# Attention logits: block-by-block weights, and exp straight from PSUM on ScalarE

## The chip, the cores and the metric

The kernel runs on one core of one Trainium2 chip. The metric is the device time of one launch in microseconds (us); smaller is better. TensorE (PE in the rows, PEld for its weight loads), VectorE (DVE), ScalarE (ACT) and GpSimd (POOL) each run their own list of instructions in order and wait for each other by semaphores. The queue that SyncE issues DMAs from is SP.

## The reference, cut to what matters

A batch of 64 images becomes 65 tokens each, 128 text tokens are joined to them (193 tokens, written L), and one attention block with relative positions and one feed-forward block follow. What the change touches is this part of the attention (8 heads, 8 channels each for q and k):

```python
rel_idx = arange(L)[:, None] - arange(L)[None, :] + (L - 1)
rpe = rel_emb[:, rel_idx]
logits = (einsum('bhdi,bhdj->bhij', q, k) + einsum('bhdi,dij->bhij', q, rpe_k)
          + einsum('bhdi,dij->bhij', k, rpe_q))
attn = softmax(logits, axis=3)
out = einsum('bhij,bhdj->bhdi', attn, v) + einsum('bhij,dij->bhdi', attn, rpe_v)
```

## The kernel before

A first stage turns the images into tokens. The second stage, `fused_block`, handles the 32 pairs of images, one pair to a turn of a loop, as a software pipeline: the table `SCHEDULE` is one list of step names that every engine walks through. In a turn, the steps "c", "a", "w2t" belong to the feed-forward of one pair, "log", "exp", "tr", "rel", "pv", "place" to the attention of the next pair, and "proj" to "gaff" (projections and their group norm) to the pair after that. A step "c" is one of 16 feed-forward slices: three matmuls of 386 columns on TensorE, a product on VectorE, two gelus on ScalarE, a sum on GpSimd, and, three slices late, two more passes on TensorE. Its first matmul waits until ScalarE has done the first gelu of the slice two before it.

The logits of a pair are made in 25 blocks. The 128 output rows of a block are 16 (image, head) pairs times 8 query rows, so both products need block-diagonal weights: `q_bd` (q of one head in 8 partitions, zeros elsewhere) and `a_bd` (q and k values spread so that each query row meets its own shift of the position table `rw`). In the kernel before, block o holds the query rows o, o+25, ..., and its weights are the slice `q_bd[:, :, o::OCT]`, which has a stride of 25 elements (100 bytes). `log` i computes blocks 2i and 2i+1 into one of two PSUM banks; VectorE takes each row's maximum and writes the difference to `lp` in SBUF; four `exp` steps on ScalarE turn `lp` into exponentials in place. Then `tr` transposes groups of four blocks on TensorE and VectorE and ScalarE copy one half each.

The block-diagonal tiles are filled by DMAs of the SP queue (`spread`): k and q are written to a DRAM scratch, 16 DMAs copy q's heads into `q_bd`, and 8 DMAs read the scratch back into the diagonal places of `a_bd`, whose other places stay zero. It starts when the step `gaff` of the turn before has written `q_f` and `k_f`. The first `log` waits for all of them.

Of the kernel before, what the change touches and what calls it, by code (L numbers as in the profile page):

```python
# [51 lines left out]
LP = 8 * OCT  # L52
RW = OCT - 1 + L
GRP = 4
# [17 lines left out]
_at = 0  # L72
for _n, _w in (("ident", P), ("ones", P), ("g8", P), ("g4", P), ("mask_r", 8), ("place", HD + HD + HD)):
    CO[_n] = (_at, _w)
    _at += _w
# [8 lines left out]
SCHEDULE = (  # L84
# [12 lines left out]
N_QS, N_AS = 16 * BH, 16 * 8  # L97
EXP_AT = (0, 8, 14, 20, OCT)


def is_first(t):
    return isinstance(t, int) and t == 0


def resident(nc, ctx):

    sb = lambda n, s: ctx.enter_context(nc.sbuf_tensor(n, s, F32))
    return dict(
        con=sb("con", [P, NCONST]),
        wq_z=sb("wq_z", [P, 192]),  # L110
        wk_z=sb("wk_z", [P, 192]),
        wv_s=sb("wv_s", [P, P]),
        vec=sb("vec", [P, 16]),
        pos_s=sb("pos_s", [P, 1 + NPATCH]),
        wg_s=sb("wg_s", [P, E]),
        b1_s=sb("b1_s", [P, NF]),
        b2_s=sb("b2_s", [P, E]),
        rv=sb("rv", [P, 2 * OCT * P]),
        w2_s=sb("w2_s", [P, NF, P]),
        rw=sb("rw", [P, RW]),  # L120
        const_in=ctx.enter_context(nc.semaphore("const_in")))
# [5 lines left out]
def patch_embed(nc, a, tok_scratch, R):  # L127

    with ExitStack() as ctx:
# [75 lines left out]
        def _(act):  # L205
# [58 lines left out]
def fused_block(nc, txt, w1, tok_scratch, u_scratch, out, R):  # L264

    with ExitStack() as ctx:
# [25 lines left out]
        gst, gst_o = (sb(n, [P, 7, 4]) for n in ("gst", "gst_o"))  # L292
        q_bd = sb("q_bd", [P, BH, LP])
        a_bd = sb("a_bd", [P, BH, LP])
        mx = sb("mx", [P, 32])
# [22 lines left out]
        bank = [ctx.enter_context(nc.psum_tensor(f"bank{i}", [P, 512], F32)) for i in range(8)]  # L318
        zb, yb, lg, pv, misc = bank[0:2], bank[2], bank[3:5], bank[5:7], bank[7]

        LN = {"1": (misc, e1, e2, rs1, rs1_t), "2": (pv[0], t1, t2, rs2, rs2_t)}

        names = """w1_in w1_hi_ready w1_split setup_dve setup_pool setup_act tok_in txt_t h_ready qk_ready v_ready
            bn mv_ready gmean gspread gvar gve grstd affine_part affine norm q_spread a_spread u_out log_ready max_done log_done
            vt v_copied exp_done tr_ready tr0_copied tr1_copied wm_done pv_done pv_ready rec_done o_part obn omv omean ospread ovar ove orstd oaff_part oaffine
            onorm h2_ready logits top_done dl_ready e_ready e1_ready p1_ready ep_tr ep_copied bcast_ready
# [53 lines left out]
        def _(sp):  # L380
# [5 lines left out]
            def spread(t):  # L386
# [40 lines left out]
        def _(pe):  # L427
# [58 lines left out]
            def attend(s, t):  # L486
# [35 lines left out]
                elif s[:3] == "log":  # L522

                    i = int(s[3:])
                    if i == 0:
                        pe.wait_ge(S["q_spread"], t * N_QS + N_QS)
                        pe.wait_ge(S["a_spread"], t * N_AS + N_AS)
                    elif i >= 2:
                        pe.wait_ge(S["log_done"], t * FILLS + i - 1)
                    for k in range(2 if 2 * i + 1 < OCT else 1):  # L530
                        o = 2 * i + k
                        dst = lg[i % 2][:, k * 256:k * 256 + L]
                        mm(dst, q_bd[:, :, o::OCT], k_f[:, 0:L], start=True, stop=False)  # L533
                        m = mm(dst, a_bd[:, :, o::OCT], rw[:, OCT - 1 - o:OCT - 1 - o + L], start=False, stop=True)  # L534
                    m.then_inc(S["log_ready"], 1)
                elif s[:2] == "tr":

                    g = int(s[2])
                    octs = range(g * GRP, min(OCT, (g + 1) * GRP))
                    pe.wait_ge(S["exp_done"], t * 4 + sum(octs[-1] >= x for x in EXP_AT))  # L540
                    for c, (j0, jn) in enumerate(JC):
                        if g == 0:
                            pe.wait_ge(S["log_done"], t * FILLS + FILLS)
                        else:
                            pe.wait_ge(S[f"tr{c}_copied"], t * NG + g)
# [21 lines left out]
                elif s[:3] == "rel":  # L567
# [7 lines left out]
                    for o in octs:  # L575
                        part = pv[g % 2][:, (o - octs[0]) * P:(o - octs[0] + 1) * P]
                        mm(part, rv_o[:, 0, o, :], pr[0][:, o, :, :], start=True, stop=False)  # L577
                        m = mm(part, rv_o[0:JC[1][1], 1, o, :], pr[1][0:JC[1][1], o, :, :],  # L578
                               start=False, stop=True)
# [36 lines left out]
        def _(dve):  # L616
# [61 lines left out]
            def reciprocal(b, t):  # L678

                dve.wait_ge(S["pv_done"], t * 2 + b + 1)  # L680
                v.reciprocal(rows(t2, b), by_row(pv[b], 256)).then_inc(S["rec_done"], 1)

            def attend(s, t):
# [33 lines left out]
                elif s == "gaff":  # L717
                    group_affine(4, gst, S["grstd"], S["affine_part"], S["affine"], GS, GB, t)
                elif s[:3] == "log":

                    i = int(s[3:])
                    w = 2 if 2 * i + 1 < OCT else 1
                    if i == 0 and not is_first(t):
                        dve.wait_ge(S["pv_ready"], t * 2)
                    src = lg[i % 2][:, :].rearrange("p (k x) -> p k x", k=2)[:, 0:w, 0:L]
                    dve.wait_ge(S["log_ready"], t * FILLS + i + 1)
                    v.tensor_reduce(mx[:, 2 * i:2 * i + w], src, AX, ALU.max).then_inc(S["max_done"], 1)  # L727
                    dve.wait_ge(S["max_done"], t * FILLS + i + 1)
                    v.tensor_tensor(lp[:, 2 * i:2 * i + w, 0:L], src,
                                    mx[:, 2 * i:2 * i + w].unsqueeze(2).broadcast_to([P, w, L]),  # L730
                                    ALU.subtract).then_inc(S["log_done"], 1)
                elif s[:2] == "tr":
# [15 lines left out]
                elif s in ("place0", "place1"):  # L748
# [86 lines left out]
        def _(act):  # L835
# [19 lines left out]
            def attend(s, t):  # L855
# [11 lines left out]
                elif s == "hkeep":  # L867
# [3 lines left out]
                    a(h2[:, :], h[:, :, :].rearrange("p b l -> p (b l)"), ACT.Copy).then_inc(S["h_kept"], 1)  # L871
                elif s[:3] == "exp":
                    k = int(s[3])
                    o0, o1 = EXP_AT[k:k + 2]
# [28 lines left out]
        def _(pool):  # L903
# [30 lines left out]

            for x in (q_bd, a_bd):
                g.memset(x[:, :, :], 0.0).then_inc(S["setup_pool"], 1)
            pool.wait_ge(S["setup_dve"], 7)
# [13 lines left out]
def shape_constants(np):  # L951
# [11 lines left out]
    put("g4", (p[:, None] // 4 == p[None] // 4) / 4.0)  # L963
    put("mask_r", p[:, None] // HD == np.arange(8)[None])
    w = np.zeros((P, 3 * HD))
    w[:, HD:2 * HD] = p[:, None] % HD == np.arange(HD)[None]
# [39 lines left out]
```

## Time and profile before

| what | value |
|---|---|
| median of 3 runs | 3876.37 us (3875.5 to 3880.21) |
| time of the profiled execution | 3886.44 us |
| its span, first to last instruction | 3884.6 us |
| mean granted TensorE clock | 0.978 of full |
| TensorE busy | 3481.7 us (90%) |
| VectorE / ScalarE / GpSimd busy | 57% / 47% / 31% |

The profiled execution took 10 us more than the median of the unprofiled runs. Busy shares are means over the whole program; which engine sets the pace of a stage is read from the rows of that stage.

### The profile page before, as it was taken

The page shows a single profiled execution, that of the slowest core. Times are in us where ns is not written, and L with a number is a line of the kernel's source. Part 1 is how long each engine was busy: PE and PEld are TensorE (multiplying, and loading weights), DVE is VectorE, ACT ScalarE, POOL GpSimd, SP SyncE. Part 2 cuts the span into 40 slices and gives each one's busy share as a digit, 9 for nine tenths or more (in the row PEclk, how much of TensorE's full clock was granted, in tenths as well). Part 3 has the DMA queues.
Part 4 walks back from the last instruction along what each step waited for, and adds up shares of the span by engine and source line. Part 5 has one row for each costly group of instructions (what it writes and reads, how often), then busy time and mean ns, then how long its engine had stood idle before and what let it go on. Part 6 is the DMA issues. An engine that isn't in the chain of part 4 may idle for free.

```text
span 3884.6 us, 66340 instructions
## 1 busy us (share of the span) xinstructions
PE 3481.7 (90%) x22496; PEld 2907.9 (75%) x22496; DVE 2225.5 (57%) x4469; ACT 1810.0 (47%) x2931; POOL 1190.5 (31%) x1192
## 2 busy tenths in 40 slices
PE   4776899999999999999999999999999999999998
PEld 3665777777777777777777777777777777787776
DVE  6884455555555555555555555555555555555554
ACT  6882244444444444444444444444444444444445
POOL 0000133332233333332233333223333333223335
PEclk9997899999999999999999999999999999999999
DMA  7761000000000000000000000000000000000000
GB/s 191 152 147 34 8 10 9 5 6 9 9 7 9 9 9 9 5 6 9 9 7 9 9 9 8 6 7 9 7 9 9 9 9 8 6 7 9 7 8 5
DMA packets 165392, 79.34 MB, mean 20 GB/s; under 512 B 81631, under 2 KB 163871, under 8 KB 165023
## 3 DMA queue, kind: packets, MB, share of 16 engines
q1 hardware_dynamic: 162946, 72.99, 9.0%
q10 hardware_dynamic: 2416, 5.97, 0.5%
q8 instruction: 17, 0.28, 0.0%
q14 instruction: 13, 0.10, 0.0%
HBM read 60.65 MB, written 14.97 MB: 19 GB/s over the span
## 4 chain that ended last, share of the span: by engine, by line
issue 56%; POOL 21%; PE 10%; DVE 2%; SPq 1%; ACT 1%; POOLq 1%; DMA 0%; ACTq 0%; DVEq 0%
POOL gelu L908 20%; PE bank L434 3%; PE bank L510 1%; PE bank L475 1%; PE bank L463 1%; POOL gst L921 1%; PE bank L533 1%; PE bank L534 1%; PE bank L469 1%; PE bank L443 1%; SPq L393 1%; POOLq L907 1%; ACT gelu L842 1%; PE bank L447 1%; PE bank L444 1%
## 5 line engine op out<-in xcount | busy, mean ns | idle before, releaser
L908 POOL TENSOR_TENSOR gelu<-gelu 128x386 f32<-128x386 f32 x1024 | 1031.0, 1015 | 2116.6 <-ACT gelu L842 2110.2
L841 ACT ACTIVATE gelu<-bank,b_s 128x386 f32<-128x386 f32 x1024 | 595.6, 582 | 1334.4 <-DVE gelu L626 1328.2
L434 PE MATMUL bank<-gelu,w_s 128*128 128x386 f32 x2048 | 832.5, 493 | 31.8 <-POOL gelu L908 28.5
L626 DVE TENSOR_TENSOR gelu<-bank,ratio 128x386 f32<-128x386 f32 x1024 | 564.1, 555 | 465.7 <-PE bank L447 459.9
L842 ACT ACTIVATE gelu<-gelu,b_s 128x386 f32<-128x386 f32 x1024 | 623.6, 609 | 0.0
L443 PE MATMUL bank<-x_hi,w_hi 128*128 128x386 f32 x1024 | 523.5, 511 | 51.5 <-ACT gelu L841 47.7
L533 PE MATMUL bank<-k_f,q_bd 128*128 128x193 f32 x1600 | 510.5, 401 | 48.4 <-DMA a_bd<-u_scratch 48.4
L533 PEld LDWEIGHTS bank<-k_f,q_bd 128*128 128x128 f32 x1600 | 463.4, 332 | 69.8 <-DMA a_bd<-u_scratch 39.8
L534 PE MATMUL bank<-rw,a_bd 128*128 128x193 f32 x1600 | 514.0, 403 | 0.0
L727 DVE TENSOR_REDUCE mx<-bank 128x2 f32<-128x386 f32 (+1 forms) x416 | 226.0, 543 | 456.0 <-PE bank L534 456.0
L534 PEld LDWEIGHTS bank<-rw,a_bd 128*128 128x128 f32 x1600 | 460.4, 336 | 0.0
L434 PEld LDWEIGHTS bank<-gelu,w_s 128*128 128x128 f32 x2048 | 364.5, 189 | 79.0 <-POOL gelu L908 54.2
L444 PE MATMUL bank<-x_hi,w_lo 128*128 128x386 f32 x1024 | 348.3, 340 | 0.0
L447 PE MATMUL bank<-x_lo,w_hi 128*128 128x386 f32 x1024 | 347.9, 340 | 0.0
L443 PEld LDWEIGHTS bank<-x_hi,w_hi 128*128 128x128 f32 x1024 | 196.0, 191 | 202.7 <-ACT gelu L841 116.1
L744 DVE TENSOR_TENSOR lp<-bank,con 128x512 f32<-128x512 f32 (+1 forms) x224 | 139.1, 633 | 340.9 <-PE bank L578 340.9
L577 PE MATMUL bank<-probs,rv 128*128 128x128 f32 x1600 | 316.9, 280 | 0.0
L578 PE MATMUL bank<-probs,rv 65*128 65x128 f32 x1600 | 316.0, 279 | 0.0
L547 PE MATMUL bank<-con,lp 128*128 128x128 f32 (+1 forms) x1600 | 227.3, 281 | 68.2 <-ACT probs L881 55.9
L881 ACT ACTIVATE probs<-bank 65x512 f32<-65x512 f32 (+1 forms) x224 | 122.1, 545 | 353.2 <-PE bank L547 353.2
L262 DVE TENSOR_TENSOR xl<-xt,xh 84x1792 fp32r<-84x1792 f32 x64 | 230.1, 3639 | 46.2 <-ACT xh L236 45.4
L547 PEld LDWEIGHTS bank<-con,lp 128*128 128x128 f32 (+1 forms) x1600 | 184.2, 143 | 95.3 <-ACT probs L881 63.3
(146 smaller groups left out, 4901.4 us busy)
## 6 DMA issues: line engine op xcount, KB each, us to landing
xt<-in_x SPq DMA_DIRECT2D x192, 196.0 KB
q_bd<-q_f SPq DMA_DIRECT2D x512, 6.2 KB
a_bd<-u_scratch SPq DMA_DIRECT2D x256, 25.0 KB, 2.2
txt_s<-in_txt SPq DMA_DIRECT2D x32, 128.0 KB, 2.2
rv<-in_rel_v ACTq DMA_DIRECT2D x1, 3200.0 KB, 18.7
u_scratch<-k_f SPq DMA_DIRECT2D x32, 100.0 KB, 2.2
u_scratch<-q_f SPq DMA_DIRECT2D x32, 100.0 KB, 2.2
out<-o_s SPq DMA_DIRECT2D x64, 48.5 KB
```

The source lines that it names most:

```text
L434: mm(yb[:, 0:T2], w2_s[:, f, :], gelu1[:, f % RING, :], start=(f == 0), stop=(f == NF - 1)).then_inc(S["w2_done"], 1)
L443: mm(z, w1_hi[:, w], x_hi[:, :], start=True, stop=False)
L444: mm(z, w1_lo[:, w], x_hi[:, :], start=False, stop=False)
L447: mm(z, w1_hi[:, w], x_lo[:, :], start=False, stop=True).then_inc(S["z_ready"], 1)
L533: mm(dst, q_bd[:, :, o::OCT], k_f[:, 0:L], start=True, stop=False)
L534: m = mm(dst, a_bd[:, :, o::OCT], rw[:, OCT - 1 - o:OCT - 1 - o + L], start=False, stop=True)
L547: m = nc.tensor.transpose(lg[c][0:jn, (o - octs[0]) * P:(o - octs[0] + 1) * P], lp[:, o, j0:j0 + jn], ident)
L577: mm(part, rv_o[:, 0, o, :], pr[0][:, o, :, :], start=True, stop=False)
L626: v.tensor_tensor(gelu2[:, f % RING, :], zb[f % 2][:, 0:T2], ratio[:, :], ALU.mult).then_inc(S["z2_done"], 1)
L841: a(gelu1[:, f % RING, :], zb[f % 2][:, 0:T2], ACT.Gelu, bias=b1_s[:, f:f + 1]).then_inc(S["g_done"], 1)
L842: a(gelu2[:, f % RING, :], gelu2[:, f % RING, :], ACT.Gelu, bias=b1_s[:, f:f + 1]).then_inc(S["g_done"], 1)
L908: g.tensor_tensor(gelu1[:, f % RING, :], gelu1[:, f % RING, :], gelu2[:, f % RING, :], ALU.add).then_inc(S["hs_done"], 1)
```

## The change

The query rows are grouped otherwise: block o now holds rows 8o to 8o+7. `q_bd` and `a_bd` are laid out as [partition, block, (image, head), row], so that the 128 weights of a block lie side by side. `rw` and `rv` get the matching tables. The DMAs for q now write pieces of 8 elements (32 bytes). The 8 DMAs for the shifted values no longer write only the diagonal: each copies all 200 columns to 16 partitions of a new tile `a_rep`, and four products on VectorE (steps `am0` to `am3`, of 7, 6, 6 and 6 blocks) multiply it with a 0/1 mask into `a_bd`. The first `log` waits for all four. The logits use four PSUM banks in place of two. VectorE computes the negated maximum only, and ScalarE computes exp from PSUM block by block with that as bias; the subtraction and the four `exp` steps are gone. In the table of steps, four "c" stand ahead of `am0`, one behind each of `am0`, `am1` and `am2`, none among the `log` steps, and two behind the last `log`.

```diff
 SCHEDULE = (
-    "c c c c c vt0 hkeep log0 log1 log2 c log3 log4 log5 c log6 log7 c log8 "
-    "exp0 log9 exp1 log10 log11 exp2 log12 exp3 c tr0 tr1 rel0 ...
+    "c c c c am0 c am1 c am2 c am3 vt0 hkeep log0 log1 log2 log3 log4 log5 log6 log7 log8 "
+    "log9 log10 log11 log12 c c tr0 tr1 rel0 ...
...
                 for bh in range(BH):
                     rows = slice(DK * bh, DK * bh + DK)
-                    sp.dma_start(q_bd[rows, bh, :], q_f[rows, :]).then_inc(S["q_spread"], 16)
+                    sp.dma_start(q_bd[rows, :, bh, :], q_f[rows, :].rearrange("p (o r) -> p o r", r=8)).then_inc(S["q_spread"], 16)
                 sp.wait_ge(S["u_out"], t * 32 + 32)
                 for r in range(8):
-                    sp.dma_start(a_bd[r:P - 7 + r:8, :, OCT * r:OCT * r + OCT],
-                                 u_scratch[:, :, :, OCT * r:OCT * r + OCT].rearrange("b s d i -> (s d) b i")).then_inc(S["a_spread"], 16)
+                    sp.dma_start(a_rep[r:P - 7 + r:8, :, :], u_scratch[:, :, :, :].rearrange("b s d i -> (s d) b i")).then_inc(S["a_spread"], 16)
...
                     if i == 0:
                         pe.wait_ge(S["q_spread"], t * N_QS + N_QS)
-                        pe.wait_ge(S["a_spread"], t * N_AS + N_AS)
-                    elif i >= 2:
-                        pe.wait_ge(S["log_done"], t * FILLS + i - 1)
+                        pe.wait_ge(S["a_masked"], t * 4 + 4)
+                    elif i >= LOGS:
+                        pe.wait_ge(S["log_done"], t * FILLS + i - LOGS + 1)
...
-                        dst = lg[i % 2][:, k * 256:k * 256 + L]
-                        mm(dst, q_bd[:, :, o::OCT], k_f[:, 0:L], start=True, stop=False)
-                        m = mm(dst, a_bd[:, :, o::OCT], rw[:, OCT - 1 - o:OCT - 1 - o + L], start=False, stop=True)
+                        dst = lt[i % LOGS][:, k * 256:k * 256 + L]
+                        mm(dst, q_bd[:, o, :, :], k_f[:, 0:L], start=True, stop=False)
+                        m = mm(dst, a_bd[:, o, :, :], rw[:, 192 - 8 * o:192 - 8 * o + L], start=False, stop=True)
...
+                elif s[:2] == "am":
+
+                    o0, o1 = (0, 7, 13, 19, OCT)[int(s[2]):int(s[2]) + 2]
+                    if s == "am0":
+                        dve.wait_ge(S["a_spread"], t * N_AS + N_AS)
+                    v.tensor_tensor(a_bd[:, o0:o1, :, :],
+                                    a_rep[:, :, 8 * o0:8 * o1].rearrange("p b (o r) -> p o b r", r=8),
+                                    K["mask_q"].unsqueeze(1).unsqueeze(1).broadcast_to([P, o1 - o0, BH, 8]),
+                                    ALU.mult).then_inc(S["a_masked"], 1)
...
-                    v.tensor_reduce(mx[:, 2 * i:2 * i + w], src, AX, ALU.max).then_inc(S["max_done"], 1)
-                    dve.wait_ge(S["max_done"], t * FILLS + i + 1)
-                    v.tensor_tensor(lp[:, 2 * i:2 * i + w, 0:L], src,
-                                    mx[:, 2 * i:2 * i + w].unsqueeze(2).broadcast_to([P, w, L]),
-                                    ALU.subtract).then_inc(S["log_done"], 1)
+                    v.tensor_reduce(mx[:, 2 * i:2 * i + w], src, AX, ALU.max, negate=True).then_inc(S["max_done"], 1)
...
-                    act.wait_ge(S["log_done"], t * FILLS + (o1 + 1) // 2)
-                    a(lp[:, o0:o1, 0:L], lp[:, o0:o1, 0:L], ACT.Exp).then_inc(S["exp_done"], 1)
+                    act.wait_ge(S["max_done"], t * FILLS + i + 1)
+                    for k in range(w):
+                        o = 2 * i + k
+                        m = a(lp[:, o, 0:L], lt[i % LOGS][:, k * 256:k * 256 + L], ACT.Exp, bias=mx[:, o:o + 1])
+                    m.then_inc(S["log_done"], 1)
```

On VectorE, in the loop's turn, these rows stood between the fourth "c" and the second `log` before (gelu<-bank,ratio is the product of a "c", the rows ISA and REGISTER_ALU only prepare waits):

```order
L626 TENSOR_TENSOR gelu<-bank,ratio 128x386
L624 REGISTER_ALU
L626 TENSOR_TENSOR gelu<-bank,ratio 128x386
L724 ISA
L726 ISA
L727 TENSOR_REDUCE mx<-bank 128x2
L729 TENSOR_TENSOR lp<-bank,mx 128x386
L726 REGISTER_ALU
L727 TENSOR_REDUCE mx<-bank 128x2
L729 TENSOR_TENSOR lp<-bank,mx 128x386
```

And these stand there now, from the fourth "c" to the first maximum:

```order
L623 TENSOR_TENSOR gelu<-bank,ratio 128x386
L720 ISA
L721 TENSOR_TENSOR a_bd<-a_rep,con 128x896
L621 REGISTER_ALU
L623 TENSOR_TENSOR gelu<-bank,ratio 128x386
L721 TENSOR_TENSOR a_bd<-a_rep,con 128x768
L621 REGISTER_ALU
L623 TENSOR_TENSOR gelu<-bank,ratio 128x386
L721 TENSOR_TENSOR a_bd<-a_rep,con 128x768
L621 REGISTER_ALU
L623 TENSOR_TENSOR gelu<-bank,ratio 128x386
L721 TENSOR_TENSOR a_bd<-a_rep,con 128x768
```

The products of the fifth, sixth and seventh "c" stand behind the first mask product, which waits for the DMAs of `a_rep`.

On TensorE, at the third and fourth `log` of the turn, this stood before (L533 and L534 are the two matmuls of a block, L443 to L434 those of a "c"):

```order
L533 MATMUL bank<-k_f,q_bd 128x193
L534 MATMUL bank<-rw,a_bd 128x193
L440 REGISTER_ALU
L443 MATMUL bank<-x_hi,w_hi 128x386
L444 MATMUL bank<-x_hi,w_lo 128x386
L447 MATMUL bank<-x_lo,w_hi 128x386
L433 REGISTER_ALU
L434 MATMUL bank<-gelu,w_s 128x386
L529 REGISTER_ALU
L533 MATMUL bank<-k_f,q_bd 128x193
```

Now the last "c" ahead of the logits, the two transposes of `vt0` and the first block stand so:

```order
L441 MATMUL bank<-x_hi,w_hi 128x386
L442 MATMUL bank<-x_hi,w_lo 128x386
L445 MATMUL bank<-x_lo,w_hi 128x386
L431 REGISTER_ALU
L432 MATMUL bank<-gelu,w_s 128x386
L479 ISA
L481 MATMUL bank<-con,e 128x128
L481 MATMUL bank<-con,e 65x128
L524 ISA
L531 MATMUL bank<-k_f,q_bd 128x193
L532 MATMUL bank<-rw,a_bd 128x193
```

All 50 matmuls of the logits follow each other with no "c" among them.

## Rows read from the trace of the kernel before

**Rows 1.** The page's head: the span and the busy times.

```profile
span 3884.6 us, 66340 instructions
PE 3481.7 (90%) x22496; PEld 2907.9 (75%) x22496; DVE 2225.5 (57%) x4469; ACT 1810.0 (47%) x2931; POOL 1190.5 (31%) x1192
```

**Rows 2.** Costliest groups of the page: count, busy us, mean ns, idle before.

```profile
L841 ACT ACTIVATE gelu<-bank,b_s 128x386 f32<-128x386 f32 x1024 | 595.6, 582 | 1334.4 <-DVE gelu L626 1328.2
...
L626 DVE TENSOR_TENSOR gelu<-bank,ratio 128x386 f32<-128x386 f32 x1024 | 564.1, 555 | 465.7 <-PE bank L447 459.9
```

**Rows 3.** TensorE's waits from 410 to 3880 us: total us, times, longest us.

```profile
PE bank L533 <- DMA a_bd<-u_scratch: 33.4, 31, 3.6
```

**Rows 4.** Timeline of the SP queue: start us, us, form, count.

```profile
2076.09 0.60 SPq L390 DMA_DIRECT2D u_scratch<-k_f  x1
...
2077.37 10.95 SPq L393 DMA_DIRECT2D q_bd<-q_f  x16
2088.44 5.15 SPq L396 DMA_DIRECT2D a_bd<-u_scratch  x8
...
2185.04 0.59 SPq L390 DMA_DIRECT2D u_scratch<-k_f  x1
```

**Rows 5.** Timeline of TensorE at the first logits: start us, us, idle before.

```profile
2095.11 0.80 PE L533 MATMUL bank<-k_f,q_bd 128*128 128x193 f32 x2 [0.87 <-DMA a_bd<-u_scratch]
2095.74 0.64 PE L534 MATMUL bank<-rw,a_bd 128*128 128x193 f32 x2
...
2100.51 0.64 PE L534 MATMUL bank<-rw,a_bd 128*128 128x193 f32 x2
2100.86 0.47 PE L443 MATMUL bank<-x_hi,w_hi 128*128 128x386 f32 x1
...
2102.16 0.56 PE L533 MATMUL bank<-k_f,q_bd 128*128 128x193 f32 x2
```

**Rows 6.** Timeline of TensorE at the projections, whose weights lie side by side.

```profile
2062.88 0.82 PE L510 MATMUL bank<-e,wk_z 128*128 128x193 f32 x4
2063.54 0.81 PE L513 MATMUL bank<-e,wv_s 128*128 128x386 f32 x2
```

**Rows 7.** Timeline of TensorE at the second group of transposes, behind the logits.

```profile
2016.02 0.66 PE L547 MATMUL bank<-con,lp 128*128 128x128 f32 x4 [0.35 <-DVE probs L736]
2018.48 0.65 PE L547 MATMUL bank<-con,lp 128*65 128x128 f32 x4 [1.81 <-ACT probs L881]
```

**Rows 8.** Stretches: us, busy per engine, granted clock, DMA share, GB/s.

```profile
2076.00:2078.50 2.50, 1.59 (x8) 1.03 (x7) 1.20 (x5) 2.50 (x7) 0.59 (x2) 1.00 0.31 81
2089.50:2094.00 4.50, 4.50 (x21) 3.27 (x20) 2.24 (x4) 4.12 (x8) 3.89 (x4) 1.00 0.34 38
100.00:200.00 100.00, 71.34 (x510) 67.29 (x509) 86.75 (x25) 87.14 (x30) 0.00 (x0) 0.91 0.74 154
```

**Rows 9.** Two waits of TensorE and what follows each, same columns.

```profile
333.50:348.40 14.90, 0.00 (x0) 0.00 (x0) 0.00 (x0) 0.85 (x3) 0.00 (x0) 0.50 0.15 19
348.40:351.90 3.50, 3.46 (x11) 3.49 (x12) 0.49 (x1) 0.00 (x0) 0.00 (x0) 0.50 0.02 5
72.00:77.80 5.80, 0.01 (x1) 0.00 (x0) 3.47 (x2) 5.80 (x3) 0.00 (x0) 0.80 0.95 219
77.80:82.20 4.40, 4.37 (x20) 4.38 (x21) 4.40 (x2) 4.40 (x3) 0.00 (x0) 0.50 0.97 197
```

**Rows 10.** VectorE's products by form: busy us, mean ns.

```profile
L744 DVE TENSOR_TENSOR lp<-bank,con 128x512 f32<-128x512 f32 x186 | 128.7, 692 | 332.8 <-PE bank L578 332.8
L646 DVE TENSOR_TENSOR e<-e 128x386 f32<-128x386 f32 x31 | 17.6, 568 | 1.1
```

**Rows 11.** Timelines of GpSimd, then VectorE, at the same moment.

```profile
2073.09 2.93 POOL L908 TENSOR_TENSOR gelu<-gelu 128x386 f32<-128x386 f32 x3
...
2073.24 0.92 DVE L674 TENSOR_TENSOR gst<-gst 128x4 f32<-128x4 f32 x1
```

**Rows 12.** Timeline of ScalarE: two activations of 193 columns out of PSUM.

```profile
2075.95 0.91 ACT L863 ACTIVATE e<-bank,gst 128x193 f32<-128x193 f32 x2
```

More of the change, by code:

```diff
@@ L52 @@
 LP = 8 * OCT
-RW = OCT - 1 + L
+RW = 2 * L - 1
 GRP = 4
@@ L72 @@
 _at = 0
-for _n, _w in (("ident", P), ("ones", P), ("g8", P), ("g4", P), ("mask_r", 8), ("place", HD + HD + HD)):
+for _n, _w in (("ident", P), ("ones", P), ("g8", P), ("g4", P), ("mask_r", 8), ("mask_q", 8), ("place", HD + HD + HD)):
     CO[_n] = (_at, _w)
@@ L292, in fused_block @@
         gst, gst_o = (sb(n, [P, 7, 4]) for n in ("gst", "gst_o"))
-        q_bd = sb("q_bd", [P, BH, LP])
-        a_bd = sb("a_bd", [P, BH, LP])
+        q_bd = sb("q_bd", [P, OCT, BH, 8])
+        a_rep = sb("a_rep", [P, BH, LP])
+        a_bd = sb("a_bd", [P, OCT, BH, 8])
         mx = sb("mx", [P, 32])
@@ L539, in attend @@
                     octs = range(g * GRP, min(OCT, (g + 1) * GRP))
-                    pe.wait_ge(S["exp_done"], t * 4 + sum(octs[-1] >= x for x in EXP_AT))
+                    if g == 0:
+                        pe.wait_ge(S["log_done"], t * FILLS + FILLS)
                     for c, (j0, jn) in enumerate(JC):
-                        if g == 0:
-                            pe.wait_ge(S["log_done"], t * FILLS + FILLS)
-                        else:
+                        if g > 0:
                             pe.wait_ge(S[f"tr{c}_copied"], t * NG + g)
@@ L576, in attend @@
                         part = pv[g % 2][:, (o - octs[0]) * P:(o - octs[0] + 1) * P]
-                        mm(part, rv_o[:, 0, o, :], pr[0][:, o, :, :], start=True, stop=False)
-                        m = mm(part, rv_o[0:JC[1][1], 1, o, :], pr[1][0:JC[1][1], o, :, :],
+                        mm(part, rv[:, (8 * o + P) * HD:(8 * o + P) * HD + P], pr[0][:, o, :, :], start=True, stop=False)
+                        m = mm(part, rv[0:JC[1][1], 8 * o * HD:8 * o * HD + P], pr[1][0:JC[1][1], o, :, :],
                                start=False, stop=True)
@@ L871, in attend @@
                     a(h2[:, :], h[:, :, :].rearrange("p b l -> p (b l)"), ACT.Copy).then_inc(S["h_kept"], 1)
-                elif s[:3] == "exp":
-                    k = int(s[3])
-                    o0, o1 = EXP_AT[k:k + 2]
-                    act.wait_ge(S["log_done"], t * FILLS + (o1 + 1) // 2)
-                    a(lp[:, o0:o1, 0:L], lp[:, o0:o1, 0:L], ACT.Exp).then_inc(S["exp_done"], 1)
+                elif s[:3] == "log":
+                    i = int(s[3:])
+                    w = 2 if 2 * i + 1 < OCT else 1
+                    if i == 0 and not is_first(t):
+                        act.wait_ge(S["pv_ready"], t * 2)
+                    act.wait_ge(S["max_done"], t * FILLS + i + 1)
[3 more added lines that the diff above has]
+                    m.then_inc(S["log_done"], 1)
                 elif s[:2] == "tr":
@@ L933, in attend @@
                     g.tensor_tensor(ep[0:GW, 0:4], half[0:GW, 1:2].broadcast_to([GW, 4]), dl[0:GW, 0:4], ALU.pow).then_inc(S["e_ready"], 1)
-            for x in (q_bd, a_bd):
-                g.memset(x[:, :, :], 0.0).then_inc(S["setup_pool"], 1)
+            g.memset(q_bd[:, :, :, :], 0.0).then_inc(S["setup_pool"], 1)
             pool.wait_ge(S["setup_dve"], 7)
@@ L984 @@
     rel = i["L0_attn_rel_emb"]
-    j_of = np.arange(P)[:, None, None, None] + P * np.arange(2)[:, None, None]
-    rel_rows = np.maximum(OCT * np.arange(8)[:, None] + np.arange(OCT) - j_of + L - 1, 0)
     arrays = {
```

27 lines of the change are left out of this document (12 added, 15 removed), and 2 rows, old and new, of the table SCHEDULE.

## The prediction

> **What bounds the kernel now.** I read the head of the page first [rows 1]: TensorE is busy for 3481.7 of 3884.6 us, the other engines for 57% at most, so over the program TensorE sets the pace. Shares are means, so I then took one turn of the loop from the SP queue's timeline: the scratch of k is written at 2076.09 us and again at 2185.04 us, a turn of 108.95 us [rows 4], and 31 such turns make most of the span. Next the timeline of TensorE at the logits [rows 5]. From 2095.74 to 2100.51 us are ten pairs of passes, two passes to an fp32 matmul, so a matmul starts every 0.477 us; the 50 of a turn take 23.9 us. Nothing waits there: the weights and columns alone set that time. Then the waits [rows 3]: once in each turn, 31 times, TensorE waits for the DMA of `a_bd` ahead of its first logit, for 0.87 us in this turn [rows 5]. So the way of the values through the SP queue is already as long as TensorE's work beside it. Whatever makes this way longer is paid in full, and that is what the reader should keep in mind beside the faster matmuls.
>
> **The change part by part**, in us per turn.
>
> *The 50 logit matmuls.* Their weights had a stride of 100 bytes and lie side by side now. The projections of q and k have the same 193 columns and weights side by side: four passes from 2062.88 to 2063.54 us, 0.165 each [rows 6], against 0.2385 for a pass of the logits. 100 passes take 16.5 in place of 23.9: a gain of 7.4. From below, the gain is nothing if the stride is not what makes them slow; I take 7.4, since size, type and engine are the same in both rows.
>
> *ScalarE and four banks.* Two exps from PSUM have to be done per `log`, which TensorE makes in 8 x 0.165 = 1.32. Two activations of that size from PSUM took 0.91 [rows 12], and the maximum on VectorE takes about 0.55, as a product of 386 columns out of PSUM does [rows 2]. Neither is slower than 1.32, and with four banks TensorE may be three `log` steps, 3.96, ahead of a chain of about 1.5. This costs nothing as long as TensorE covers it; if exp took 0.7 apiece, the logits would run at ScalarE's pace and lose 13 x 0.1 = 1.
>
> *The wait at the second transposes.* TensorE stood for 0.35 and 1.81 there, 2.16 in all [rows 7], since ScalarE had its last long exp, a change of function and two gelus ahead of its copy. Now two "c" stand there. The second covers another 1.30 (the step from 2100.86 to 2102.16 us [rows 5]), but puts two more gelus of 0.58 [rows 2] ahead of the copy, while the exp left over at the end is short. That gives back between nothing and 2.16; I take 0.8.
>
> *The DMAs of q.* 16 issues took 10.95 [rows 4], and their 8 partitions x 25 blocks make 200 pieces of 32 bytes each. The nearest row is that of the old `a_bd` DMAs, 256 pieces of 100 bytes: a DMA share of 0.34 at 38 GB/s [rows 8] is 38/(0.34 x 16) = 7.0 GB/s per busy engine, 14.3 ns apiece. 200 pieces on 16 engines are 0.18, on 8 engines 0.36, under the 0.68 between issues. I take nothing. The upper bound is pieces that cost as much as 800 bytes in the scratch's write: 81/(0.31 x 16) = 16.3 GB/s, 49 ns [rows 8]; on 8 engines that is 1.23 per DMA, 16 x (1.23 - 0.68) = 8.7 in all.
>
> *The DMAs of `a_rep`.* Each moves 16 x 16 rows of 800 bytes, 204.8 KB in place of 25.6. The eight are issued within 5.15 [rows 4], but 1.638 MB have to move. At the rate of the image loads, 154 GB/s at a share of 0.74, that is 208 GB/s [rows 8] and 7.9; at the rate of the scratch's write, 81/0.31 = 261 GB/s, 6.3. The last old one is issued at 2088.44 + 7 x 0.644 = 2092.95 and TensorE starts at 2095.11 [rows 4, 5], 2.16 behind, of which 0.23 is transfer (256 pieces of 14.3 ns on 16 engines). The new ones land at 2088.44 + 1.9 + 7.9 = 2098.2, 3.1 later than before; at the better rate 1.5 later. I take 3.1, since the image loads too write a part of the partitions.
>
> The Trainium skill's page "SBUF — State Buffer" (section "Door 1: The DMA port swizzle") says that a DMA's rate goes by how many of 16 ports its partitions reach, 27.2 GB/s each; by its table, partitions r, r+8, ..., r+120 reach 8. That rule speaks against this change and gives 218 GB/s, an estimate of 7.5 and a landing 2.7 later, where the row gave 3.1; no row here has this pattern of partitions with long pieces.
>
> *The mask products.* Products of 386 and 512 columns take 0.568 and 0.692 [rows 10], about 1 ns per column more, so 896 columns take 1.08 and 768 take 0.95: 3.9 for the four. On VectorE the products of the fifth, sixth and seventh "c" stand among them, 3 x 0.5: together 5.4 from landing to the first logit. They also meet GpSimd's sums: a product of 4 elements took 0.92 while GpSimd ran its sums [rows 11], each about 1.0, so a product with both inputs in SBUF waits until GpSimd's instruction ends. Two of the four can be hit, by the sums of the fifth and sixth "c": 0 to 2, I take 1.2. The first logit starts at 2098.2 + 6.6 = 2104.8.
>
> The same page (section "SBUF: two separate sides") calls the pair of ports that VectorE and GpSimd share an exclusive lock, held for a whole instruction. By that rule GpSimd is held back in turn, and the sixth "c"'s sum could go behind a mask product; the sum stays within my 0 to 2.
>
> *What is queued behind that wait.* VectorE stands at `am0` with the fifth "c" behind it; TensorE can do the fifth and sixth, but the seventh needs the fifth's gelu. Before, the fifth "c" and `vt0` were done 0.87 ahead of 2095.11; a sixth lasts until about 2095.5. Then TensorE has nothing until about 2.4 after the landing, does the seventh, and stands again until 2104.8. Two "c", 2 x 1.30, are now done ahead of the logits, so the 9.7 by which the first logit moves cost 9.7 - 2.6 = 7.1. With the better DMA rate and no sums in the way it is 4.3; with the bound for q's pieces 15.8.
>
> *The clock.* From 2095.5 to 2104.8 us TensorE now works for 1.5 and stands for 7.8. In both waits of comparable or greater length that I list the granted clock was down when work came back: after 14.9 idle it was 0.50 for the first 3.5, after 5.8 idle 0.50 for 4.4 [rows 9], the lower of its two levels, 1.2 GHz. The logits would start at it. A pass of 193 columns is then bound by its columns, so half of some 4.4 is lost: 2.2. Nothing from below, 3.2 from above.
>
> *Sum.* -7.4 - 0.8 + 7.1 + 2.2 = +1.1 per turn, times 31 = +34 us. The first turn has no "c" and pays 3.1 + 3.9 for a gain of 7.4 less the low clock: nothing to speak of. The profiled execution, 3886.4 us, would become 3920; its 10 us over the median 3876.4 taken off, 3910.
>
> **The rivals.**
>
> *The way through the queue grows less, or the clock holds* (faster). Then the matmuls win. With 7.1 and no loss of clock the sum is -1.1, 34 us faster, 3842. With 4.3 and 1.0 for the clock it is -2.9, 90 us faster, 3786. For it: the rate of 261 GB/s is there in the trace, and a wait of 1.81 in every turn leaves the mean clock at 0.978. Against it: the new wait is longer than that one, and the masks cannot start ahead of the last byte. It decides in favour of the change where delay and clock together stay under 8.2.
>
> *Pieces of 32 bytes choke the queue.* At 49 ns on 8 engines the landing moves by another 8.7; at half of the excess 4.3. The sum is +5.4 to +9.8, 167 to 304 us slower, 4045 to 4180. For it: pieces are 25 times as many. Against it: 100-byte pieces ran at 14.3 ns.
>
> *The stride is not what slows the logits.* Then the 7.4 are gone, and the turn loses 8.5 at most: 264 us, 4140. Rows 6 speak against it.
>
> **How the numbers follow.** A measurement of this kernel tells 0.2%, 8 us, from no change. My forecast, a delay that eats the gain, has 0.50, its own range 3860 to 3975; within it 0.08 fall inside 0.2% and 0.02 on the fast side. The faster rival has 0.34, of which 0.01 is within 0.2%. Choked queue 0.11, stride without effect 0.05. Faster: 0.02 + 0.33 = 0.35; same: 0.09; slower: 0.40 + 0.11 + 0.05 = 0.56. The range 3800 to 4000 leaves out about 0.05 of the fastest and 0.13 of the slowest cases.
>
> **What the profile of the changed kernel would show.** Pairs of logit passes 0.33 apart, weight loads no longer as long as a pass. SP's sixteen issues still in 11 us. `am0` starting 22 us after the scratch's write, in place of 19 to the first logit. A wait of TensorE for VectorE ahead of the first logit, and one ahead of the seventh "c" for ScalarE, some 8 us together, with a low clock behind them. Masks near 1 us each, up to 1.9 where GpSimd is in its sum. The wait at the second transposes down to about 1.4. I am wrong if `am0` comes no later than 19 us after the write, if the clock stays up, or if ScalarE, not TensorE, sets the pace of the logits.

## The result, and the profile after

The changed kernel takes 3900.5 us (median of 4 runs, 3891.3 to 3909.3) against 3878.3 us before (4 runs, 3875.5 to 3880.6): ratio 1.0057, 95% interval 1.0032 to 1.0083. It is slower by 22 us or 0.6%, 0.7 us for each of 31 turns. The forecast was 3910 and slower. The profiled execution is the fastest of the four, 3891.3 us with a span of 3889.4. That is 4.8 us over the span of before, whose profiled execution (3886.4 us) was slower than all four of its timed ones.

Head and some groups of the page of the changed kernel (`a_rep` in part 6: KB each, median us from issue to landing):

```profile
span 3889.4 us, 66829 instructions
PE 3295.7 (85%) x22496; PEld 2686.9 (69%) x22496; DVE 2164.7 (56%) x4181; ACT 1953.9 (50%) x3603; POOL 1197.8 (31%) x1191
...
L881 ACT ACTIVATE lp<-bank,mx 128x193 f32<-128x193 f32 x800 | 292.2, 419 | 253.3 <-DVE mx L731 253.3
...
L721 DVE TENSOR_TENSOR a_bd<-a_rep,con 128x768 f32<-128x768 f32 (+1 forms) x128 | 161.7, 1265 | 234.4 <-DMA a_rep<-u_scratch 234.4
...
a_rep<-u_scratch SPq DMA_DIRECT2D x256, 200.0 KB, 4.7
```

TensorE does the same 22496 matmuls in 186 us less busy time than in [rows 1], and the program is not faster: the gain has become waiting. The waits of TensorE in the turns show where (answers to [rows 3]: us in all, times, longest us):

```profile
PE bank L441 <- ACT gelu L841: 264.6, 153, 8.5
...
PE bank L531 <- DVE a_bd L721: 35.1, 31, 1.2
...
PE bank L544 <- ACT probs L887: 21.6, 31, 0.7
```

L441 is the first matmul of a "c". Its large wait comes once in each turn, at the seventh "c". The queue's timeline of one turn, which answers to [rows 4]:

```profile
2080.80 0.59 SPq L389 DMA_DIRECT2D u_scratch<-k_f  x1
...
2082.07 11.89 SPq L392 DMA_DIRECT2D q_bd<-q_f  x16
2094.09 5.15 SPq L395 DMA_DIRECT2D a_rep<-u_scratch  x8
```

VectorE in the same turn, from the fourth "c" to the last mask:

```profile
2097.15 0.56 DVE L623 TENSOR_TENSOR gelu<-bank,ratio 128x386 f32<-128x386 f32 x1 [0.62 <-PE bank L445]
2104.46 1.09 DVE L721 TENSOR_TENSOR a_bd<-a_rep,con 128x896 f32<-128x896 f32 x1 [6.75 <-DMA a_rep<-u_scratch]
2105.47 0.56 DVE L623 TENSOR_TENSOR gelu<-bank,ratio 128x386 f32<-128x386 f32 x1
2105.93 0.95 DVE L721 TENSOR_TENSOR a_bd<-a_rep,con 128x768 f32<-128x768 f32 x1
2106.80 0.56 DVE L623 TENSOR_TENSOR gelu<-bank,ratio 128x386 f32<-128x386 f32 x1
2107.27 1.77 DVE L721 TENSOR_TENSOR a_bd<-a_rep,con 128x768 f32<-128x768 f32 x1
2108.97 0.55 DVE L623 TENSOR_TENSOR gelu<-bank,ratio 128x386 f32<-128x386 f32 x1
2109.44 1.28 DVE L721 TENSOR_TENSOR a_bd<-a_rep,con 128x768 f32<-128x768 f32 x1
```

GpSimd's sums of the fifth and sixth "c" meanwhile (its timeline):

```profile
2107.22 1.01 POOL L914 TENSOR_TENSOR gelu<-gelu 128x386 f32<-128x386 f32 x1 [7.23 <-ACT gelu L842]
2108.56 1.35 POOL L914 TENSOR_TENSOR gelu<-gelu 128x386 f32<-128x386 f32 x1 [0.33 <-ACT gelu L842]
```

And TensorE, which answers to [rows 5]:

```profile
2106.69 0.69 PE L441 MATMUL bank<-x_hi,w_hi 128*128 128x386 f32 x1 [6.66 <-ACT gelu L841]
...
2110.87 0.56 PE L531 MATMUL bank<-k_f,q_bd 128*128 128x193 f32 x2 [1.13 <-DVE a_bd L721]
2111.27 0.49 PE L532 MATMUL bank<-rw,a_bd 128*128 128x193 f32 x2
2111.59 0.49 PE L531 MATMUL bank<-k_f,q_bd 128*128 128x193 f32 x2
...
2127.14 0.48 PE L441 MATMUL bank<-x_hi,w_hi 128*128 128x386 f32 x1
```

The reader is to see the chain: VectorE stands 6.75 us for the last bytes of `a_rep`, with the fifth "c" behind it; TensorE stands 6.66 us for that slice's gelu, and another 1.13 us for the last mask. Then 50 matmuls take 16.27 us, 0.327 apart. From the scratch's write to the first logit are 30.07 us (2080.80 to 2110.87), where 19.02 were. The turn is a usual one: over the 31 turns with a "c" the means are 30.2 and 19.2.

### The profile page after: what moved, and what is told of

Its sections match the earlier page's. It is cut to its first block, busy times and chain, and to the rows that moved or that the text cites. A ratio compares the mean times of both kernels' runs of the same rounds, so it can differ in the third digit from the quotient of the medians.

```text
span 3889.4 us, 66829 instructions
## 1 busy us (share of the span) xinstructions
PE 3295.7 (85%) x22496; PEld 2686.9 (69%) x22496; DVE 2164.7 (56%) x4181; ACT 1953.9 (50%) x3603; POOL 1197.8 (31%) x1191
## 4 chain that ended last, share of the span: by engine, by line
issue 56%; POOL 21%; PE 10%; DVE 2%; SPq 1%; ACT 1%; POOLq 1%; DMA 0%; ACTq 0%; DVEq 0%
POOL gelu L914 20%; PE bank L432 3%; PE bank L508 1%; PE bank L473 1%; PE bank L461 1%; POOL gst L927 1%; PE bank L467 1%; SPq L392 1%; PE bank L441 1%; ACT gelu L842 1%; POOLq L913 0%; PE bank L445 0%; PE bank L442 0%; DVE gelu L623 0%; PE bank L531 0%
## 5 line engine op out<-in xcount | busy, mean ns | idle before, releaser
L432 PE MATMUL bank<-gelu,w_s 128*128 128x386 f32 x2048 | 855.3, 504 | 33.6 <-POOL gelu L914 30.1
L441 PE MATMUL bank<-x_hi,w_hi 128*128 128x386 f32 x1024 | 542.9, 530 | 265.9 <-ACT gelu L841 264.6
L441 PEld LDWEIGHTS bank<-x_hi,w_hi 128*128 128x128 f32 x1024 | 196.5, 192 | 441.8 <-ACT gelu L841 353.4
L531 PE MATMUL bank<-k_f,q_bd 128*128 128x193 f32 x1600 | 405.2, 336 | 58.3 <-DVE a_bd L721 58.3
L432 PEld LDWEIGHTS bank<-gelu,w_s 128*128 128x128 f32 x2048 | 374.4, 194 | 82.3 <-POOL gelu L914 57.4
L881 ACT ACTIVATE lp<-bank,mx 128x193 f32<-128x193 f32 x800 | 292.2, 419 | 253.3 <-DVE mx L731 253.3
L532 PE MATMUL bank<-rw,a_bd 128*128 128x193 f32 x1600 | 401.7, 334 | 0.0
L531 PEld LDWEIGHTS bank<-k_f,q_bd 128*128 128x128 f32 x1600 | 289.7, 195 | 70.0 <-issue 70.0
L721 DVE TENSOR_TENSOR a_bd<-a_rep,con 128x768 f32<-128x768 f32 (+1 forms) x128 | 161.7, 1265 | 234.4 <-DMA a_rep<-u_scratch 234.4
L532 PEld LDWEIGHTS bank<-rw,a_bd 128*128 128x128 f32 x1600 | 290.9, 195 | 0.0
```

The costliest lines, as they stand in the source:

```text
L432: mm(yb[:, 0:T2], w2_s[:, f, :], gelu1[:, f % RING, :], start=(f == 0), stop=(f == NF - 1)).then_inc(S["w2_done"], 1)
L441: mm(z, w1_hi[:, w], x_hi[:, :], start=True, stop=False)
L531: mm(dst, q_bd[:, o, :, :], k_f[:, 0:L], start=True, stop=False)
L532: m = mm(dst, a_bd[:, o, :, :], rw[:, 192 - 8 * o:192 - 8 * o + L], start=False, stop=True)
```

## The experiments

All twelve are told. Times are medians; each ratio is to the kernel before, timed in the same job (3874.1, 3876.8 and 3875.0 us in the three jobs). The changed kernel was not timed again in them, and beside its 3900.5 us the kernel before took 3878.3. So a difference to the changed kernel can be off by some 4 us from that alone: by the ratios, the 28, 18 and 2 us of masks_last, q_whole and warm are 23, 16 and nothing.

**w_side.** The kernel before with weights side by side alone.

```diff
-mm(dst, q_bd[:, :, o::OCT], k_f[:, 0:L], ...)
-m = mm(dst, a_bd[:, :, o::OCT], rw[...], ...)
+mm(dst, q_bd[:, :, :].rearrange("p b l -> p (b l)")[:, P * o:P * o + P], k_f[:, 0:L], ...)
+m = mm(dst, a_bd[:, :, :].rearrange("p b l -> p (b l)")[:, P * o:P * o + P], rw[...], ...)
```

> The kernel before with one edit: the logit matmuls read 128 weights that lie side by side (a flat slice of the same tiles, so the logits are not the reference's; everything else runs as before). Theory A (the stride is what slows them, and the changed kernel loses the gain again elsewhere): matmuls 0.33 us apart instead of 0.477, 7.5 us less per turn, less up to 1.3 since two banks with maximum and subtraction take about as long per step as TensorE: 190 to 230 us faster, 3650 to 3690 us. Rival (stride without effect): 3878 us, no change.

Measured 3681.7 us, ratio 0.9498 [0.9483, 0.9514], 192 us faster. The stride is what made the matmuls slow. TensorE at the logits of this kernel:

```profile
2095.62 0.49 PE L534 MATMUL bank<-rw,a_bd 128*128 128x193 f32 x2
2095.95 0.49 PE L533 MATMUL bank<-k_f,q_bd 128*128 128x193 f32 x2
2096.27 0.49 PE L534 MATMUL bank<-rw,a_bd 128*128 128x193 f32 x2
2096.70 0.59 PE L533 MATMUL bank<-k_f,q_bd 128*128 128x193 f32 x2
```

Matmuls are 0.327 apart within a step, but 0.43 apart where a step begins, about 0.1 us a step or 1.3 us a turn. With two banks TensorE waits there for maximum and subtraction, as I read it; with four banks and no subtraction (both_old_dmas) the gap is gone.

**exp_psum.** The kernel before with the other half alone; the DMAs and the strided weights stay.

```diff
-"c c c c c vt0 hkeep log0 log1 log2 c log3 ... exp0 log9 ... exp3 c tr0 ..."
+"c c c c c c c vt0 hkeep log0 log1 log2 log3 ... log12 c c tr0 ..."
+LOGS = 4;  lt = bank[3:7]      # and maximum, exp and waits as in the changed kernel
```

> The kernel before with the other half alone: negated maximum, exp from PSUM block by block with it as bias, four banks, no 'c' among the logit steps (seven ahead, two behind), old weights and old DMAs. Theory A: costs nothing on TensorE, since ScalarE and VectorE are under its pace; the wait of 0.87 us for the DMAs and half of the wait of 2.16 us at the second transposes go: 1 to 2 us per turn, 30 to 60 us faster, 3820 to 3850 us. Rival (ScalarE's 25 exps cost time): over 3880 us.

Measured 3801.9 us, 0.9815 [0.9799, 0.9832], 72 us faster, more than I expected. The waits show both sources: that for the DMAs, 33.4 us in [rows 3], is 1.0 us here, since two "c" more stand ahead of the logits, and that for ScalarE's copy, 55.9 us before, is 16.4 (us in all, times, longest). The two together are 71.9 us less.

```profile
PE bank L547 <- ACT probs L880: 16.4, 31, 0.5
```

**both_old_dmas.** The two together, with the old DMAs: weights side by side out of `q_bd` and `a_bd` as the old DMAs fill them.

> w_side and exp_psum together on the kernel before, with its old DMAs (the logits are not the reference's): the whole change without the longer way to a_bd. Theory A (the halves add and the loss is all in the way): 3874 - 192 - 72, about 3610 us; with the way for the DMAs, 19 us, now closer to TensorE's work beside it, up to 30 us more: 3600 to 3650 us. Rival (with both, ScalarE or VectorE sets the pace of the logits): 3700 us or more.

Measured 3559.7 us, 0.9184 [0.9167, 0.9201], 315 us faster, 51 more than the two alone. Most of these 51 is the 0.1 us a step of w_side, 1.3 us a turn, that is gone here: all 50 matmuls are 0.33 apart. This is what the change is worth without a longer way, 10.2 us a turn. The changed kernel is 341 us slower than this. In the traces nearly all of it is the way from the scratch's write to the first logit, 30.2 us a turn against 20.4; some 16 us are a low clock at the logits (see warm).

**few_bytes.** The changed kernel with an eighth of the bytes in its `a_rep` DMAs (and `a_rep` cleared once at the start).

```diff
-sp.dma_start(a_rep[r:P - 7 + r:8, :, :], u_scratch[:, :, :, :]...)
+sp.dma_start(a_rep[r:P - 7 + r:8, :, OCT * r:OCT * r + OCT], u_scratch[:, :, :, OCT * r:OCT * r + OCT]...)
```

> The changed kernel, but each of the eight DMAs into a_rep moves only 25 of the 200 columns (the pieces of the kernel before; the shifted values are incomplete, so the logits are not the reference's). Masks, order and number of DMAs stay. Theory A (bytes delay the landing): the masks start 3.5 us earlier, the turn loses 3 to 3.6 us: 3790 to 3810 us. Rival (clock decides: the stretch at the lower level stays and eats it): 3860 us or more. Rival (masks and issues alone set the delay): 3900 us.

Measured 3802.6 us, 0.9811 [0.9793, 0.9829], 98 us less than the changed kernel. From issue to landing in one turn, as the view of the tile `a_rep` gives it:

```profile
DMA to landing us min/median/max: 2.2/2.3/2.3
```

In the changed kernel the same line of `a_rep` reads:

```profile
DMA to landing us min/median/max: 3.2/4.6/5.9
```

The last landing moves by the difference of the longest, 3.6 us, and most of it, 3.2 us a turn, comes back. The rival of the clock holds a part of the rest: in the trace the logits of 22 of the 31 turns now begin at the lower level (6 in the changed kernel), and the logits take 0.8 us more on average.

**no_masks.** The changed kernel without the four products.

```diff
-"c c c c am0 c am1 c am2 c am3 vt0 ..."
+"c c c c c c c vt0 ..."
-pe.wait_ge(S["a_masked"], t * 4 + 4)
+pe.wait_ge(S["a_spread"], t * N_AS + N_AS)
-m = mm(dst, a_bd[:, o, :, :], rw[...], ...)
+m = mm(dst, a_rep[:, :, :].rearrange("p b l -> p (b l)")[:, P * o:P * o + P], rw[...], ...)
```

> The changed kernel without the four mask products; the first logit waits for the DMAs of a_rep and its weights are read from a_rep directly (not block-diagonal, so the logits are not the reference's). Theory A (masks and the feed-forward products among them are 6.4 us of the way to the first logit): 5.5 to 6.5 us less per turn, 3700 to 3730 us. Rival (the clock's low stretch then falls on the logits instead of on the wait and gives back 2 us of it): 3760 to 3790 us.

Measured 3729.9 us, 0.9628 [0.9612, 0.9644]: 171 us less, 5.5 a turn, at the slow end of what I gave theory A and below the rival's range. What the rival named is there, but smaller than its 2 us: the way to the first logit is 6.3 us shorter in the trace (23.9 against 30.2), and 0.65 goes back since the logits of 20 of 31 turns begin at the lower level.

**q_whole.** The changed kernel, with q's pieces whole.

```diff
-sp.dma_start(q_bd[rows, :, bh, :], q_f[rows, :].rearrange("p (o r) -> p o r", r=8))
+sp.dma_start(q_bd[rows, :, :, :].rearrange("p o b r -> p (o b r)")[:, LP * bh:LP * bh + LP], q_f[rows, :])
```

> The changed kernel, with the 16 DMAs of q writing one whole piece of 800 bytes per partition as before (to the wrong places of the block-by-block tile, so the logits are not the reference's). Theory A (the small pieces cost only the 0.95 us by which the 16 issues take longer, 11.9 instead of 10.95): up to 0.95 us less per turn, 3865 to 3900 us. Rival (they also hold up the landing of a_rep behind them): 3 us or more per turn, 3800 us or less.

Measured 3882.0 us, 1.0016 [1.0006, 1.0026], 18 us less than the changed kernel. The 16 issues take the old time again (the queue's timeline):

```profile
2079.99 10.93 SPq L392 DMA_DIRECT2D q_bd<-q_f  x16
```

The first logit comes 0.9 us earlier, as the issues do, so the small pieces cost their slower issue and no more; the rival of a choked queue is out. A part goes back to the clock: in the trace the logits of 14 turns begin at the lower level, and over all turns they take 0.4 us more.

**warm.** The changed kernel with work of no use in TensorE's long wait.

```diff
+elif s == "am2":
+    for _ in range(24):
+        mm(lt[3][:, 0:P], ident, ident, start=True, stop=True)
```

> The changed kernel, and in the long wait of TensorE ahead of the seventh 'c' 24 small matmuls of constants into an unused PSUM bank, about 5.3 us, so that the granted clock has less of a wait to fall in; nothing else changes. Theory A (in the usual turn the low stretch ends before the first logit, so it costs nothing; only the few turns with twice as long a stretch pay): 0 to 30 us faster than the changed kernel, 3870 to 3900 us. Rival (the low clock costs 2.2 us in every turn, as I forecast): 3830 to 3840 us.

Measured 3898.4 us, 1.0056 [1.0039, 1.0074], no different from the changed kernel. In the profiled execution the mean granted clock rose from 0.952 to 0.984, and the median stayed. The stretches of the changed kernel show why it is worth so little (us, busy of each engine, then the clock): in this turn it is low while TensorE does the seventh "c", and full again when the logits begin. Nobody waits for that "c": at full clock in warm it is followed by a wait of 2.5 us for the last mask where 1.1 were, and the first logit stands 30.2 us behind the write in both.

```profile
2106.70:2110.20 3.50, 3.04 (x7) 1.92 (x7) 3.50 (x5) 2.18 (x5) 2.36 (x2) 0.50 0.04 11
2110.90:2127.10 16.20, 16.20 (x99) 16.20 (x100) 6.44 (x12) 9.84 (x25) 0.82 (x1) 1.00 0.00 0
```

In some turns it stays low longer. In the turn before this one the first logits run at the lower level, 0.645 us apart (TensorE's timeline, then the stretch):

```profile
1999.88 0.85 PE L532 MATMUL bank<-rw,a_bd 128*128 128x193 f32 x2
2000.52 0.85 PE L531 MATMUL bank<-k_f,q_bd 128*128 128x193 f32 x2
2001.17 0.85 PE L532 MATMUL bank<-rw,a_bd 128*128 128x193 f32 x2
...
2000.00:2004.40 4.40, 4.40 (x16) 4.40 (x15) 0.56 (x1) 1.65 (x3) 0.00 (x0) 0.50 0.00 0
```

That is so in 6 of the 31 turns. In each the logits take 2.5 to 2.7 us more than in the others, and these six turns are the longest of the trace (111.7 to 112.2 us; no other is over 110.0): 16 us in all, or 0.5 a turn. The trace of warm has three such turns of 1.7 us each, and its execution is 9 us faster than the profiled one of the changed kernel. So the low level costs a little, and not the 2.2 us a turn of the rival. Why warm's median is not lower is not shown: its four slower runs have a lower mean clock (0.978 to 0.980), and no trace.

**masks_last.** The changed kernel with one edit in the table.

```diff
-"c c c c am0 c am1 c am2 c am3 vt0 ..."
+"c c c c c c c am0 am1 am2 am3 vt0 ..."
```

> The changed kernel with one edit in the table of steps: all seven 'c' ahead of am0, the four masks in one row behind them. DMAs as in the changed kernel. Theory A (the three feed-forward products among the masks, and GpSimd's sums that they set off, lie on the way to the first logit; TensorE has done its seven 'c' before the landing): the way from landing to first logit is 4.0 instead of 6.4 us: 3810 to 3840 us. Rival (the wait is as long as before, only in one piece): 3890 us.

Measured 3872.3 us, 0.9997 [0.9987, 1.0007], 28 us less than the changed kernel where 60 to 90 were expected. The way did shorten, to 27.4 us in the turn I looked at: scratch write at 2066.76, masks in one row, first logit at 2094.14. But here the low level falls on the logits (TensorE's timeline):

```profile
2094.14 0.98 PE L531 MATMUL bank<-k_f,q_bd 128*128 128x193 f32 x2 [6.76 <-DVE a_bd L721]
...
2099.42 0.55 PE L531 MATMUL bank<-k_f,q_bd 128*128 128x193 f32 x2
```

The stretch of these matmuls (us, busy time of each engine, then the granted clock):

```profile
2094.10:2099.00 4.90, 4.86 (x15) 4.89 (x16) 0.56 (x1) 0.74 (x2) 0.00 (x0) 0.50 0.00 1
```

Eight matmuls take 5.28 us in place of 2.62: 2.7 us, as much as the shorter way gave in that turn. It is so in all 31 turns: on average the way is 2.5 us shorter and the logits take 1.8 us longer. So the step that I had charged to the changed kernel exists, in the kernel whose wait lies whole ahead of its logits.

**rep_first.** The changed kernel with another order of issues in the SP queue.

```diff
-for bh in range(BH): ...                 # 16 DMAs of q
+q_heads(0, 3)
 sp.wait_ge(S["u_out"], t * 32 + 32)
 for r in range(8): ...                   # 8 DMAs of a_rep
+q_heads(3, BH)
```

> The changed kernel with one change of order in the SP queue: three of q's DMAs, then the eight of a_rep, then q's other thirteen. All bytes, masks and steps are the same. Theory A (it is the way from the scratch's write to the masks that costs, and the two kinds of DMA can run beside each other): a_rep lands some 14 us behind the write instead of 23.7, am0 waits for nothing and TensorE's wait of 6.7 us goes: 3690 to 3740 us, faster than both kernels. Rival (the bytes of a_rep hold up q's DMAs as long in this order): 3850 us or more.

Measured 3657.2 us, 0.9434 [0.9412, 0.9456], faster than both kernels by 5.7 and 6.2%, and better than expected. `am0` waits for nothing. q's thirteen are issued at the usual pace while the bytes of `a_rep` are still landing (10.9 us after their first issue, 10.5 in the changed kernel), so the two kinds of transfer do run beside each other (the queue's timeline):

```profile
2068.26 5.14 SPq L397 DMA_DIRECT2D a_rep<-u_scratch  x8
2073.44 9.62 SPq L393 DMA_DIRECT2D q_bd<-q_f  x13
```

What is left of the wait is the last mask, 1.5 us a turn (TensorE's waits: us in all, times, longest):

```profile
PE bank L534 <- DVE a_bd L724: 45.0, 31, 1.5
```

**rep_first_masks_early.** The same, and the masks two slices earlier.

```diff
-"c c c c am0 c am1 c am2 c am3 vt0 ..."
+"c c am0 c am1 c am2 c am3 c c vt0 ..."
```

> rep_first, and the mask steps two 'c' earlier (am0 behind the second 'c', two 'c' behind am3). Theory A: with the masks out of the way the last DMA of q, some 20.5 us behind the write, is the end of the way, about as long as TensorE's own work beside it: all of the faster matmuls is kept, 3600 to 3660 us. Rival (the masks delay the feed-forward products on VectorE by about 1 us each wherever they stand): 3690 to 3720 us, like rep_first.

Measured 3638.2 us, 0.9385 [0.9364, 0.9406], the fastest of the kernels that compute all of it. TensorE's timeline at the first logit, where it no longer waits:

```profile
2079.33 0.38 PE L484 MATMUL bank<-con,e 128*128 128x128 f32 x2
2079.54 0.49 PE L534 MATMUL bank<-k_f,q_bd 128*128 128x193 f32 x2
```

78 us are left to both_old_dmas, and the first logit comes 2.3 us later behind the write (22.6 against 20.4). The rival may hold this part, the masks delaying the slices among which they stand; no run separates it.

**before_a_first.** The kernel before with the same order of issues (`a_bd` ahead of thirteen of q's).

> The kernel before with the order of rep_first in its SP queue (three of q's DMAs, the eight of a_bd, thirteen of q). Theory A (all 26 DMAs are needed by the first logit, so the order of issues cannot shorten the way; only the wait for the scratch's write can go): 3860 to 3880 us, no gain like that of rep_first. Rival (the order alone helps any kernel): 3840 us or less.

Measured 3882.0 us, 1.0021 [1.0011, 1.0030], no gain, even 7 us more, for which no row gives the cause. Its wait for the DMAs is now for q's last one (22.7 us in 31 turns). The order alone does not help; it helped where bytes and masks stand behind it.

**two_banks.** rep_first_masks_early with two banks.

```diff
-LOGS = 4
+LOGS = 2
-lt = bank[3:7]
+lt = bank[3:5]
```

> rep_first_masks_early with two PSUM banks for the logits in place of four. Theory A (a step of the logits is 1.31 us on TensorE, and maximum and two exps behind it take about 1.5 with the hand-overs, so with two banks TensorE waits some 0.4 us at each of 12 steps, plus once for ScalarE's change of function): 5 to 8 us more per turn, 3790 to 3890 us. Rival (the banks are not needed): 3640 us.

Measured 3743.7 us, 0.9656 [0.9639, 0.9674]: 106 us more, 3.4 a turn, less than my 5 to 8, but far from nothing. With exp on ScalarE two banks are not enough; three were not tried.

## Why the prediction was right, step by step

The total was right, and the main mechanism: the faster logits are paid back by a longer way from the scratch to `a_bd`, which both_old_dmas and rep_first show from both sides. One term, the clock, was not. Of its terms, in us per turn:

| term | forecast | measured |
|---|---|---|
| 50 logit matmuls | -7.4 | -7.6 (50 x 0.477 less 16.27) |
| wait at the second transposes | -0.8 | -1.1 (2.16 to 0.35 + 0.69) |
| first logit later | 9.7 | 11.05 |
| two "c" now ahead of it | -2.6 | -2.4 (1.18 apart) |
| low clock | +2.2 | 0 in this turn, 0.5 on average |
| sum | +1.1 | -0.05 in this turn, the turn itself 108.95 to 109.12, +0.17; +0.7 over the medians |

*Matmuls, ScalarE, banks.* Right. Two exps took 0.73 us together against 1.31 for a step; ScalarE waits 0.57 us in each step for the maximum. w_side shows the stride as the cause, two_banks that "costs nothing" does not hold with two.

*The DMAs of q.* I took nothing; the term is 0.94 (11.89 against 10.95). My argument from the pieces' own time was right, since their landing holds up nothing, but the queue takes 0.06 us longer for each issue. In the kernel before, DMAs of 8 pieces and of 256 had been issued at nearly the same pace, 0.684 and 0.644, and so I left it out.

*The DMAs of `a_rep`.* I took 3.1 from the image loads' 208 GB/s; it was 3.7 (10.37 from first issue to `am0`, against 6.67 to the first logit before). The rate of the scratch's write, 261 GB/s, would have given 1.5: the choice of the row was right, and its size 0.6 short. The Trainium skill's rule of ports ("SBUF — State Buffer", section "Door 1: The DMA port swizzle") gave 2.7; the trace agrees with its direction and is 1.0 longer. few_bytes shows that it is the bytes.

*Masks.* 6.4 from landing to first logit, 6.6 forecast: 1.09 and 0.95 us as worked out, and two of four stretched, to 1.77 and 1.28, while GpSimd was in a sum. It was held back in turn, as the prediction allowed: the sum that began during the mask of 1.77 took 1.35 in place of 1.01. no_masks shows 5.5 of them.

*The clock.* This step failed. I charged 2.2 us since the level was low after two long waits, and did not ask what work meets it. In 25 of 31 turns it is low while TensorE does the seventh "c", with no one waiting, and back at full for the logits. In the other six it takes about 2.6 us, 0.5 a turn in all, and warm's medians show no more than that for the program as a whole. The kernel before pays as much elsewhere: nine of its turns have a low stretch behind the logits, where the changed kernel has none, and take 110.6 to 112.6 us against 108.9 to 109.2 for the others, 0.7 a turn. That the total came out close is in part luck: the way with its two "c" cost 8.65 where I had charged 7.1, 1.55 too little, and the 2.2 charged for the clock, nearly all of it too much, made up for that.

*Rivals.* The choked queue and the stride without effect are refuted. The faster case asked for delay and clock under 8.2; the clock cost little, but the delay alone was 8.65.

What stays open is the step from the ledger of a turn to the medians: +0.17 a turn would be 5 us, as the two profiled executions differ, and the medians say 22. The other 17 us are where the profiled executions lie: that of before 8 us above its median, that of the changed kernel 9 us below its own. Why one kernel's executions differ so much is not shown. The four of the changed kernel spread over 18 us, those of before over 5. Turns whose low level lasts into the logits are a candidate, since the slower runs have the lower mean clock (0.947 to 0.949 against 0.952); those of warm (3882 to 3903 us) have it too, but of either kernel only the fastest run has a trace.

## What to carry to other kernels

A matmul that gets faster only shortens the side of a fork that TensorE is on; look first at what runs beside it, and how long its slack is. Here the slack was less than nothing (a wait of 0.87 us), and the same edit brought the means of the gain (weights side by side) and the bill (bytes and masks behind sixteen other issues). Order the issues of a queue by how much work stands behind each transfer: the one with bytes and masks behind it first, those that only have to land last. That one change of order was worth 243 us.

A low granted clock costs only the work that meets it and that someone waits for. Ask which instructions fall into it before charging it, and look at every turn: few_bytes, no_masks and masks_last each had their logits at the lower level in more turns than the changed kernel.

## What the runs showed of the hardware

- Weights at a stride of 100 bytes made an fp32 matmul of 193 columns take 0.477 us in place of 0.327. A weight load took 336 ns on average, and 195 with the weights side by side.
- DMAs inside SBUF in pieces of 32 bytes were issued 0.743 us apart, those in pieces of 800 bytes 0.684, though 256 pieces of 100 bytes out of DRAM went at 0.644.
- Two exps of 193 columns out of PSUM with a bias each took 0.73 us, and each of the two lasted 0.42. Two calls of 193 columns so cost ScalarE 0.15 us more than one of 386 (0.58, a gelu).
- A mask product of 768 columns took 0.95 us alone and 1.28 to 1.77 beside a sum on GpSimd; a sum of 1.01 us took 1.35 beside it.
- Filling TensorE's wait with work of no use raised the mean clock from 0.952 to 0.984 in the profiled executions and left the median where it was (3898 against 3900 us).
- Eight matmuls that met the lower clock took 5.28 us in place of 2.62.
